# One core, four layers: the FFN's residual on ScalarE, and a new order of the SSM's first and last steps

## What is computed

```python
x = x + attn_a(_layernorm(x), w_qkv, w_proj, b_proj)
x = x + ffn(_layernorm(x), ...)
x = x + attn_b(_layernorm(x), W_in, conv_w, ...)      # the SSM
x = x + ffn(_layernorm(x), ...)

def ffn(x, ...):                                     # x is the layernormed input
    t = x * rsqrt(mean(x * x) + EPS) * scale
    g = t @ gate_w.T + gate_b
    route = softmax over the top 4 of g, 0 elsewhere
    acc = sum_e route[:, e] * (swiglu(t @ w1[e].T + b1[e]) @ w2[e].T + b2[e])
    return x + acc
```

## Time and profile before

| | us |
|---|---|
| median of 3 runs (lowest, highest) | 730.05 (729.69, 730.87) |
| the profiled execution, its own time | 729.9 |
| its span | 728.2 |
| PE busy | 707.1, 97% |
| DVE busy | 626.2, 86% |
| ACT busy | 573.4, 79% |
| POOL busy | 243.4, 33% |

### The profile page before, as it was taken

One profiled execution on the slowest core, in us unless ns is written; L12 is line 12 of the kernel. 1 busy time (PEld: TensorE's weight loads), 2 busy tenths in 40 slices (PEclk: granted clock), 3 DMA queues, 4 the chain that ended last, 5 costly groups with the idle time before them and its releaser, 6 DMA issues. The chain is left out here.

```text
span 728.2 us, 13033 instructions
## 1 busy us (share of the span) xinstructions
PE 707.1 (97%) x3800; PEld 575.9 (79%) x3800; DVE 626.2 (86%) x1503; ACT 573.4 (79%) x1095; POOL 243.4 (33%) x389
## 2 busy tenths in 40 slices
PE   6899999999999999999999999999999999999998
PEld 4688787888788877778888888888778887887886
DVE  3578886999999999967689999899769989998996
ACT  2676777988988899767787787787678889888885
POOL 2355464000015200015767767767740000610000
PEclk9999999999999999999999999999999999999999
DMA  9000012654555445400000000000146555654651
GB/s 273 5 2 3 9 33 88 219 196 156 179 188 193 166 167 180 140 0 2 1 1 1 4 3 1 9 4 1 32 174 211 177 196 190 199 196 168 224 195 53
DMA packets 29380, 77.19 MB, mean 106 GB/s; under 512 B 4899, under 2 KB 9726, under 8 KB 29310
## 3 DMA queue, kind: packets, MB, share of 16 engines
q1 hardware_dynamic: 28980, 76.29, 30.8%
q10 hardware_dynamic: 330, 0.08, 0.1%
HBM read 73.73 MB, written 2.62 MB: 105 GB/s over the span
## 5 line engine op out<-in xcount | busy, mean ns | idle before, releaser
L707 ACT ACTIVATE s_ring<-ps,b1T 128x512 f32<-128x512 f32 x256 | 171.5, 688 | 34.6 <-PE ps L1695 33.4
L1168 DVE SCALAR_TENSOR_TENSOR s_ring<-s_ring,top_col,r_all 128x1024 f32<-128x1024 f32 x128 | 166.0, 1297 | 18.4 <-ACT s_ring L707 17.8
L1180 DVE TENSOR_TENSOR s_lo<-s_ring,s_hi 128x1024 fp32r<-128x1024 f32 x126 | 153.8, 1220 | 3.8 <-ACT s_hi L713 3.8
L713 ACT ACTIVATE s_hi<-s_ring 128x1024 fp32r<-128x1024 f32 x128 | 135.1, 1055 | 9.3 <-DVE s_ring L1168 8.4
L1669 PE MATMUL ps<-s_hi,w_hi 128*128 128x512 f32 x256 | 101.5, 397 | 1.8 <-DVE s_lo L1180 1.7
L1693 PE MATMUL ps<-ffn_hi,w_hi 128*128 128x512 f32 x256 | 103.3, 404 | 0.0
L1671 PE MATMUL ps<-s_hi,w_lo 128*128 128x512 f32 x256 | 101.3, 396 | 0.0
L1695 PE MATMUL ps<-ffn_hi,w_lo 128*128 128x512 f32 x256 | 101.1, 395 | 0.0
L1694 PE MATMUL ps<-ffn_lo,w_hi 128*128 128x512 f32 x256 | 101.0, 395 | 0.0
L1670 PE MATMUL ps<-s_lo,w_hi 128*128 128x512 f32 x256 | 100.8, 394 | 0.0
L523 POOL TENSOR_TENSOR ramp<-upto,dt_a 128x512 f32<-128x512 f32 x32 | 33.0, 1043 | 83.0 <-PE ps L1671 71.5
(11 more groups left out here) (263 smaller groups left out, 1550.5 us busy)
## 6 DMA issues: line engine op xcount, KB each, us to landing
r_all<-route_dram SPq DMA_DIRECT2D x128, 512.0 KB, 3.8
out_dram<-X SPq DMA_DIRECT2D x7, 256.0 KB, 4.3
X<-in_L_attn_a_x_dram SPq DMA_DIRECT2D x1, 1536.0 KB, 9.5
rows_f<-route_dram SPq DMA_DIRECT2D x48, 32.0 KB, 2.9
w_rows<-in_L_ffn_mlp_w_dram SPq DMA_DIRECT2D x1, 1024.0 KB, 6.8
route_dram<-route_cols SPq DMA_DIRECT2D x64, 8.0 KB, 1.5
X<-in_L_attn_a_x_dram SPq DMA_DIRECT2D x2, 256.0 KB, 4.9
ssm_rows<-in_L_attn_b_W_in_dram SPq DMA_DIRECT2D x1, 384.0 KB
```

The costliest lines, as they stand in the source:

```text
L707: eng.activation(s_ring[q % NR][:, e % 2, :], bank(e % 4), ACT.Silu, bias=b1T[:, e:e + 1], scale=ALPHA).then_inc(F["act"], 1)
L713: eng.activation(s_hi[q % NR][:, :, :], s_ring[q % NR][:, :, :], ACT.Copy).then_inc(F["hi"], 1)
L1168: eng.scalar_tensor_tensor(out=s_ring[q % NR][:, :, :], in0=s_ring[q % NR][:, :, :], scalar=top_col[:, 0:1], in1=r_all[q % NR][:, :, :], o ...
L1180: eng.tensor_tensor(s_lo[q % NR][:, :, :], s_ring[q % NR][:, :, :], s_hi[q % NR][:, :, :].bitcast(F32), ALU.subtract).then_inc(F["lo"], 1)
```

## The change

1. **router_xn is dropped from DVE.** router_chain keeps two columns for each sequence in res_col: 1 + rstd and -mean * rstd, in 11 small operations instead of nine. A new function on ACT, residual, makes the residual of batch b in X at (b, q = 1) of each FFN with four Identity instructions that take these two columns as scale and bias. add_sum waits for it. router_norm waits for the seventh operation of the chain instead of its last.
2. **First SSM steps on ACT.** seg_exp(0, 0) and seg_exp(0, 1) run at the start of step -1, ahead of xs_silu; decays(0, 0) runs in step 0 behind xb_out(0, 0) instead of at the end of step -1.
3. **Last SSM step.** hidden(F2, 0, 0) moves on PE behind y_skip(7, 0), hidden(F2, 0, 1) behind xb_turn(7, 3), into banks 7 and 6. router_norm(R2, 5) moves on DVE ahead of norms(6, 3). ACT does silu 0 to 3 in the step, DVE weigh 0 and 1. g_turn(7, 1..3), gT_out(7, 2..3), out_proj, x3_out and the router's last parts move to later pairs of FFN 2's batch 0.
4. vec_row gives up its own memory and uses attn's.

```diff
+            vec_row = attn[:, 0:2, :].rearrange("p r d -> p (r d)")[0:1, 0:160]
...
+        def h_bank(F, b, e):
+            return bank(7 - e if F is F2 and b == 0 and e < 2 else e % 4)
...
-                wait(eng, R["xn"], NT * b)
+                wait(eng, R["t0"], NT * b)
...
-                tt(rt_small[:, 7, :], rt_small[:, 1, :], ones[:, 0:NT], ALU.add)
-                eng.tensor_tensor(rt_small[:, 8, :], rt_small[:, 1, :], rt_mv[:, :, 0], ALU.mult).then_inc(R["pool"], 1)
+                tt(res_col[:, b, 0, :], rt_small[:, 1, :], ones[:, 0:NT], ALU.add)
+                tt(rt_small[:, 7, :], rt_small[:, 1, :], mhalf4[:, :], ALU.mult)
+                tt(rt_small[:, 8, :], rt_small[:, 7, :], rt_mv[:, :, 0], ALU.mult)
+                eng.tensor_tensor(res_col[:, b, 1, :], rt_small[:, 8, :], rt_small[:, 8, :], ALU.add).then_inc(R["pool"], 1)
...
+            def residual(R, b):
+                eng.wait_ge(R["pool"], 11 * (b + 1))
+                eng.wait_ge(R["t0"], NT * (b + 1))
+                for r in range(NT):
+                    eng.activation(X[:, b, r, :], X[:, b, r, :], ACT.Identity, bias=res_col[:, b, 1, r:r + 1],
+                                   scale=res_col[:, b, 0, r:r + 1]).then_inc(R["xn"], 1)
...
             def late_router(R, F, b, q):
+                if q == 1 and b < NB:
+                    residual(R, b)
...
-                if (b, q) == (0, 0) and F is F2:
-                    gT_out(NB - 1, NT - 1)
-                elif (b, q) == (0, 4) and F is F2:
+                if b == 0 and q in (1, 2) and F is F2:
+                    gT_out(NB - 1, q + 1)
+                elif (b, q) == (0, 6) and F is F2:
                     router_out(R, NB - 3, bank(5))
...
+                if i == -1:
+                    seg_exp(0, 0)
+                    seg_exp(0, 1)
+                if second and i > 0:
                     seg_exp(i, 0)
                     seg_exp(i, 1)
+                if second:
                     xb_out(i, odd, 0)
+                if i == 0:
+                    decays(0, 0)
...
-                    silu(F2, 0, 0)
-                    silu(F2, 0, 1)
+                    for e in range(4):
+                        silu(F2, 0, e)
...
-                if first:
+                if first and i >= 0:
                     decays(i + 1, 1 - odd)
...
+                wait(eng, R["pool"], 11 * b)
...
-                wait(eng, R["pool"], 9 * b + 9)
+                wait(eng, R["pool"], 11 * b + 7)
...
-            def router_xn(R, b):
...
+                eng.wait_ge((R1 if F is F1 else R2)["xn"], NT * (b + 1))
...
+                if not first:
+                    router_norm(R2, i - 2)
                 if third:
                     norms(i - 1, 3)
-                if fourth:
+                if fourth and first:
                     router_norm(R2, i - 2)
-                    router_xn(R2, i - 2)
...
                     weigh(F2, 0, 0)
+                    weigh(F2, 0, 1)
...
-                        eng.wait_ge(M["xb"], NT * NB)
-                        eng.wait_ge(M["cb"], NT * NB)
-                    elif e < 3:
+                        eng.wait_ge(M["raw"], NB)
+                        eng.wait_ge(M["conv"], 6 * NB)
+                    elif e == 1:
+                        eng.wait_ge(M["xs"], 3 * NB)
+                        eng.wait_ge(M["conv"], 6 * NB)
+                    elif e == 2:
                         eng.wait_ge(M["segs"], NT * NB)
                     else:
                         eng.wait_ge(M["y"], NT * NB)
...
-                        g_turn(NB - 1, NT - 1)
-                elif (b, q) == (0, 2) and F is F2:
+                elif b == 0 and 1 <= q <= 3 and F is F2:
+                    g_turn(NB - 1, q)
+                elif (b, q) == (0, 4) and F is F2:
                     out_proj(NB - 1, 4)
...
                     y_skip(i, odd, 0)
+                if not first:
+                    eng.wait_ge(R2["stash"], 1)
+                    hidden(F2, 0, 0)
...
+                    if not first:
+                        hidden(F2, 0, 1)
                     y_skip(i, odd, 2)
```

More of the change, by code:

```diff
@@ L706, in silu @@
                 wait(eng, F["lo"], NQ * (b + done(F)) + q + 1 - NR)
-                eng.activation(s_ring[q % NR][:, e % 2, :], bank(e % 4), ACT.Silu, bias=b1T[:, e:e + 1],
+                eng.activation(s_ring[q % NR][:, e % 2, :], h_bank(F, b, e), ACT.Silu, bias=b1T[:, e:e + 1],
                                scale=ALPHA).then_inc(F["act"], 1)
@@ L735, in ffn @@
                             split(F, 0, 0)
-                        for e in (2 * q, 2 * q + 1):
-                            silu(F, b, e)
+                        if F is F1 or (b, q) != (0, 1):
+                            for e in (2 * q, 2 * q + 1):
+                                silu(F, b, e)
                         if q and (b, q) != (0, 1):
@@ L1013, in step @@
                     xs_silu(i + 1, 1 - odd)
+                if second and first:
+                    gT_out(i, 2)
                 if second:
-                    gT_out(i, 2)
                     square(i, 3)
@@ L1315, in late_router @@
                     softplus(0, 0, 1)
-                elif (b, q) == (0, 3):
-                    if F is F1:
-                        x1_out(NB - 1, 4)
-                    else:
-                        x3_out(NB - 1, 4)
+                elif (b, q) == (0, 3) and F is F1:
+                    x1_out(NB - 1, 4)
+                elif (b, q) == (0, 5) and F is F2:
+                    x3_out(NB - 1, 4)
                 elif (b, q) == (1, 2):
                     router_norm(R, NB - 2)
-                elif (b, q) == (1, 6):
-                    router_xn(R, NB - 2)
                 elif (b, q) == (2, 2):
@@ L1692, in hidden @@
                         eng.wait_ge(M["y"], NT * NB)
[L1693 to L1695 removed]
+                elif F is F2 and b == 0 and e == 4:
+                    eng.wait_ge(M["xb"], NT * NB)
+                    eng.wait_ge(M["cb"], NT * NB)
+                elif F is F2 and b == 0 and e == 5:
+                    eng.wait_ge(M["segs"], NT * NB)
+                eng.matmul(h_bank(F, b, e), w1_hi[:, e, :], ffn_hi[:, b, :], start=True, stop=False)
+                eng.matmul(h_bank(F, b, e), w1_hi[:, e, :], ffn_lo[:, b, :], start=False, stop=False)
+                eng.matmul(h_bank(F, b, e), w1_lo[:, e, :], ffn_hi[:, b, :], start=False, stop=True).then_inc(F["h"], 1)
             def ffn(F, b, peeled, tail=False, after_pair=None):
@@ L2039, in step @@
                     y_gram(i, 3)
-                if not first:
-                    eng.wait_ge(R2["stash"], 1)
-                    hidden(F2, 0, 0)
-                    hidden(F2, 0, 1)
-                if second:
+                if second and first:
                     g_turn(i, 1)
```

27 lines of the change are left out of this document (8 added, 19 removed).

## The result

The changed kernel takes 744.18 us (743.09 to 745.01, 5 runs) against 729.72 (729.50 to 730.87) of the kernel before: ratio 1.0183, 95% interval 1.0163 to 1.0203. It is slower by 14.5 us, where 5.85 were forecast.

A forecast was written before the change was run, and what follows sets the result against it. The prediction took the steady parts to be bound by PE's own list of matmuls. Its terms, 7.4 + 0.6 - 0.8 + 0.65 - 2.0, gave +5.85 us and a time of 735.9, range 729.0 to 739.5.

The forecast's parts named there:

- waits before the b2 matmul, less the s_lo waits that shrink: Both FFNs: late acc_out makes PE wait 14 times, +7.4 us; smaller PE waits for s_lo give -0.8.
- F1 batch 0: First FFN's peeled batch 0: the residual delays the second split while the pipeline fills, +0.6 us (0 to 1.36).
- first SSM step: Two more table loads on ACT; decays delays u_out and z_proj: +0.65 us (-0.3 to +1.5).
- last SSM step and start of F2: Earlier router_norm and experts filling PE's waits outweigh new waits: -2.0 us (-4.3 to +0.5).
- GpSimd's longer chain: Router chain grows from 9 to 11 small operations; nobody on PE's path waits: 0 (at most 0.3 in six steps).
- vec_row in attn's memory is read before attn is written: 0: Moving vec_row into attn's memory causes no wait, since it is read before attn is written: 0 us.
- acc_out term: FFN batches: residual makes acc_out 0.70 us later, 0.24 free; PE waits 0.46 per ordinary batch, 0.97 in batches 3.
- rival 4: Residual on ACT: each instruction costs 0.39 us, four 1.56, adding 2.8 us; time 738.7, chance 0.10.
- 0.24 + 0.13 + 0.53: ACT's room per ordinary FFN batch: acc_out's free lateness, time regained by a non-waiting pair, idle plus overlap; 0.90 us.
- Rival 1: FFN: four residual instructions fit in 0.90 us, 0.225 each, so no ordinary batch waits; time 728.2, chance 0.15.
- 2: Rival, halfway: residual instructions cost 0.25 us each, 0.10 wait per ordinary FFN batch; time 730.5, chance 0.13.
- rival 3: FFN: ACT runs out, 94% busy; backlog makes waits for s_lo grow 0.5 to 1 in six batches; 739.5, chance 0.14.

The follow-up runs named there:

- e9_res_half: Changed kernel with two of the four residual instructions left at q=1 and two moved to q=4: 736.65 us, ratio 1.0091.
- e6_both: Changed kernel with the residual at q=4 and the columns' operations at the end of GpSimd's part of an SSM step: 732.68 us, ratio 1.0027.
- e5_vec_alias: Kernel before with only vec_row moved into attn's memory: 731.83 us, ratio 1.0015.
- e2_cols_late: Changed kernel with the four GpSimd operations for the residual's columns moved to the end of the SSM step: 738.58 us, ratio 1.0114.
- e12_both_place: Kernel of e6_both with res_col in a buffer at vec_row's old place, so other buffers keep their old addresses: 732.07 us, ratio 1.0015.
- e11_alias_pad: Kernel of e5_vec_alias with an unused buffer left at vec_row's place, so every other buffer has its old address: 731.61 us, ratio 1.0006.
- e7_both_first_old: Kernel of e6_both with ACT's old order in the first SSM step: 733.43 us, ratio 1.0047.
- e13_all_old_order: Kernel of e6_both with the old orders of both the first and the last SSM step: 733.21 us, ratio 1.0028.
- e8_both_last_old: Kernel of e6_both with the last SSM step and start of the second FFN in the old order on all engines: 732.65 us, ratio 1.0028.
- e16_rows_xn_later: Kernel before with both the later rows_split and the later last-step router_xn, nothing of the change: 730.38 us, ratio 0.9984.
- e15_rows_later: Kernel before with GpSimd's rows_split(F2) in the last SSM step moved behind rms(7,3): 729.05 us, ratio 0.9970.
- e14_xn_later: Kernel before with DVE's router_xn(R2, 5) moved from the last SSM step to (0,5) of the second FFN: 730.00 us, ratio 0.9992.
- e1_res_q4: Changed kernel with all four residual instructions moved to q=4, behind acc_out: 736.73 us, ratio 1.0085.
- e3_pool_plus2: Kernel before with two small unread operations added at the end of GpSimd's router chain: 735.91 us, ratio 1.0073.
- e10_before_again: Kernel before, unchanged, profiled once more: 730.30 us, ratio 0.9996.

## Why the prediction was wrong

The direction and most terms were right; the sum was +5.85 and the span grew by 13.7. The terms with what the runs make of them, in us; each is a difference of the same stretch in two profiles:

| term | forecast | measured | from |
| --- | --- | --- | --- |
| waits before the b2 matmul, less the s_lo waits that shrink | +6.6 | +6.8 | changed kernel against e9_res_half, both FFNs from batch 0 to 7 and the stretch to out_proj(0), less the 0.7 of the next row |
| F1 batch 0 | +0.6 | +0.7 | the same pair: from batch 0 to 1 it is 1.21 longer, from an ordinary batch to the next 0.52 |
| first SSM step | +0.65 | +0.8 | e6_both against e5_vec_alias, F1 batch 7 to out_proj(0): 55.84 and 55.07; they differ in the residual too |
| last SSM step and start of F2 | -2.0 | -1.7 | the same pair, out_proj(5) to F2 batch 1: 75.04 and 76.71 |
| GpSimd's longer chain | 0 | +4.3 | changed kernel against e2_cols_late, out_proj(0) to (6) |
| addresses of the buffers | 0 | +1.3 | e6_both against e12_both_place, both FFNs |
| start and attention | 0 | +1.5 | changed kernel; the unchanged one had +1.3 in its second profile |

Together 13.7. Two things are left out of it, about 0.5 each and opposite: e9_res_half is itself longer than e5_vec_alias by 0.32 in F1 and 0.24 in batches 1 to 7 of F2, and the first profile of the kernel before has 24.20 us between F1's batches 5 and 6 where its second has 23.77. So the account is good to half a microsecond, not better.

**The step that failed** is the sentence "POOL's chain grows from 9 to 11 small operations; it has idle time behind it and nobody on PE's path waits: 0 (at most 0.3 in six steps)". The idle time is real, 33% busy on the page, but it lies in front of other operations. Directly behind the chain stand gate and fade with no slack, DVE's states waits for fade, and DVE's gn for g_turn on PE stands behind states. Moving the four operations of the columns away from that place gave 4.3 us back, and adding two to the kernel before cost 3.4. The question that I asked of the engine (is it idle?) had to be asked of the instruction behind the insertion: who waits for it, and how long has it been done by then. PE has no idle time in the step in which to make it up, so that each steady step pays anew.

**The second miss** is "vec_row in attn's memory is read before attn is written: 0". True of the dependences, but the move shifts every buffer behind it, and in each of the four kernels compared for it (e5_vec_alias and e6_both with shifted addresses, e11_alias_pad and e12_both_place with the old ones) the pace of PE's matmuls goes with the addresses.

**The acc_out term** was right in mechanism and nearly in size: 0.52 us per ordinary batch, 0.46 forecast. Two errors met in it. An instruction takes 0.39 us on ACT, not 0.34, as rival 4 had it. The estimate worked out from the figures of the Trainium skill (ScalarE: Activation LUTs, What ACT_TABLE_LOAD costs) is 0.386, and this trace agrees with its 1.55 for four; I had let the plain copy's 0.16 speak against it. That copy reads PSUM, and so do the attention's instructions of 128x128 with one column (L647), which start 0.25 apart; a second column at the 0.09 that the forecast took for each would make 0.34. The residual reads SBUF. That its source makes the difference of 0.05 is a guess: no run moved it. By the forecast's arithmetic 1.55 gives 0.65 per batch. Measured are 0.52, so there was 0.13 more room than the 0.24 + 0.13 + 0.53 that I had added up. Rival 1 (the residual hides) and 2 fell with the 0.39; that its threshold exists is shown by e9_res_half. Of rival 3 (ACT runs out) nothing was seen: 144.03 of 160 us is 90%, where the forecast had near 94%, and from 560 us on PE waits 0.3 us for s_lo where it was 0.7.

**The first SSM step** went as worked out: three table loads, each 1.28 us, with the next instruction 0.01 to 0.02 behind:

```profile
326.35 1.28 ACT L956 ACT_TABLE_LOAD   x1
327.65 1.09 ACT L956 ACTIVATE segs<-ps 128x512 f32<-128x512 f32 x2
328.75 1.28 ACT L791 ACT_TABLE_LOAD   x1
330.05 1.58 ACT L791 ACTIVATE xs<-conv_acc 128x512 f32<-128x512 f32 x2
```

What I had not seen is that the one wait of 1.57 us would break into three of 0.62, 0.77 and 1.00 us. The size is less sure than the mechanism: both profiles with the old order and the residual on ACT (e7_both_first_old, e13_all_old_order) have the drop of the clock, so that no stretch at a clock of 1.0 isolates the new order.

**The last SSM step** was right in size for a wrong reason. I credited the new order with the gain: experts that fill PE's waits. Its signs came: no wait before router_turn, and new waits of 0.8 (before a hidden, L1718) and 1.3 us (before the first ffn_out, L1681), the 2.1 that the forecast had. But e8_both_last_old has the old order and the same time. The gain is mostly DVE's: no router_xn there, and router_norm beside little of rows_split (1.40 us in e8_both_last_old) or none (1.83 in e6_both, where its first instruction starts beside GpSimd's ramp). e16_rows_xn_later, with nothing but these two, gains 1.3 of the 1.7; the rest is for the most part the longer wait for gn named there (1.1 us, and 0.8 in e8_both_last_old). The earlier trace rows had the clue, 2.13 us for four instructions, and I took it for their price; the same four take 1.11 in e15_rows_later.

## What to carry to other kernels

Idle share says nothing about an insertion; look at what stands directly behind it on the same engine and who waits for that, also when the engine is busy for a third of the time. Ahead of an instruction that the bounding engine needs at once, count the room: what fits is free, what doesn't is paid in every iteration, and moving the work behind that instruction costs one line. And when an operation takes twice its usual time in one place, look at what the neighbouring engine does at that moment before you take it for its price.

## What the runs showed of the hardware

**DVE beside GpSimd.** Four tensor_scalar of 128x128 on DVE take 1.11 us alone and 2.13 with GpSimd's cast and subtraction beside them. The Trainium skill (SBUF — State Buffer, SBUF: two separate sides) describes a port pair shared by the two, held by one instruction at a time, so that the other blocks; this case agrees. Taking the neighbour away removed the lengthening, and in the kernel before the four instructions of the earlier trace rows come apart:

```profile
513.44 1.26 POOL L474 TENSOR_TENSOR rows_r<-rows_f,rows_r 16x512 fp32r<-16x512 f32 x1
513.43 1.36 DVE L1075 TENSOR_SCALAR t<-X,rt_mv,rt_small 128x128 f32<-128x128 f32 x1
514.71 0.85 DVE L1075 TENSOR_SCALAR t<-X,rt_mv,rt_small 128x128 f32<-128x128 f32 x3
```

The first of the four takes 1.36 us instead of 0.34 and lasts until GpSimd's subtraction has ended, and the other three then start 0.26 apart, as in e15_rows_later. GpSimd's subtraction takes 1.26 us beside them and 1.28 alone. So one instruction held the other up for its whole length; the two did not both go slower.

**Addresses and the pace of matmuls.** Ordinary FFN batches without a wait take 24.30 us in the kernel before (twice), e11_alias_pad, e12_both_place, e14_xn_later, e15_rows_later and e16_rows_xn_later, which have the old addresses, and 24.39 to 24.42 in e1_res_q4, e3_pool_plus2, e5_vec_alias, e6_both, e7_both_first_old, e8_both_last_old, e9_res_half and e13_all_old_order, which have not. Over the 700 or so neighbouring starts of each profile in F2, one start to the next is 0.2321 against 0.2336 us (0.2333 in e3_pool_plus2, whose buffers are shifted by 32 bytes); the figures in the expectations above are a little lower. Which buffer it is, and why, stays open.

**A drop of the clock behind a wait.** In six of ten profiles with the old order of the first SSM step the granted clock falls from 2.4 to 1.2 GHz within 2 us of the end of the 1.57 us wait; in none of the seven with the new order does it fall in this stretch. The windows of e10_before_again:

```profile
320.00:328.00 8.00, 7.51 (x39) 5.43 (x37) 2.81 (x6) 5.13 (x8) 0.00 (x0) 1.00 0.00 0
328.00:332.00 4.00, 2.68 (x14) 2.71 (x14) 1.80 (x5) 2.66 (x12) 2.62 (x3) 0.68 0.00 0
332.00:336.00 4.00, 4.00 (x24) 3.39 (x25) 1.81 (x6) 1.66 (x6) 2.02 (x3) 0.89 0.00 0
```

The stretch to the first out_proj takes 56.3 to 56.4 us in such profiles of kernels like the one before, and 57.9 in e3_pool_plus2, instead of 55.1; with the new order it takes 55.8 whenever it was profiled with the residual at q=4. That would make the two orders equal on average, and fits that e13_all_old_order is no faster than e8_both_last_old; the count of profiles is too small to call it shown. Nor does the new order keep the clock up over a whole execution: 21 of the 58 executions of the kernels with it have a mean clock below 0.999, and 96 of 197 with the old one. The profile of e1_res_q4 has its drop at 23 us, in the attention; where those of the executions without a profile lie, nothing here shows.
